# Queries stacked through DRAM instead of by transposes of split copies, with a new place for the first norm's statistics and the first score pair

## The reference

```
h = layernorm(x);  q = relu(h), k = v = relu(ctx)          # 16 heads of 32 features
att = softmax(q k^T / sqrt(32));  z = relu(att v @ ffn_w.T + ffn_b)
x1 = x + tanh(g_xattn) * z
n = layernorm(x1);  xr, xk = mixes of n and n shifted by one position (mu_r, mu_k)
y = sigmoid(xr @ W_r.T) * (relu(xk @ W_k.T)^2 @ W_v.T)
out = x1 + tanh(g_ffn) * y
```

## Time and profile before

| | us |
|---|---|
| median of 3 runs | 2914.57 (2912.64 to 2914.85) |
| the profiled execution's own time | 2913.12 |
| its span, first to last instruction | 2911.3 |
| steady time of one item | 44.20 |

### The profile page before, as it was taken

How to read it: one execution, slowest core, us unless ns; L and a number is a source line. 1 busy time by engine, 2 the same in 40 slices (tenths; PEclk the granted TensorE clock), 3 DMA queues, 4 the chain that set the end, 5 groups by cost and what they waited for, 6 DMA issues and landing times.

```text
span 2911.3 us, 71226 instructions
## 1 busy us (share of the span) xinstructions
PE 2792.9 (96%) x23042; PEld 2158.7 (74%) x23042; DVE 2367.5 (81%) x4173; ACT 1631.3 (56%) x2955; POOL 1055.1 (36%) x902
## 2 busy tenths in 40 slices
PE   4899999999999999999999999999999999999998
PEld 3677777777777777777777777777777777777776
DVE  5788888888888888888888888888888888888874
ACT  4555656556556555555556565565565555555552
POOL 0234334333333333343343343333333333333434
PEclk9999999999999999999999999999999999999999
DMA  5544544544544544545445445445445444454431
GB/s 183 151 142 133 158 140 132 159 140 135 152 145 131 157 132 142 149 131 152 142 130 159 139 133 159 139 135 152 143 132 157 132 144 146 132 154 141 130 112 43
DMA packets 405369, 408.83 MB, mean 140 GB/s; under 512 B 164560, under 2 KB 329424, under 8 KB 405328
## 3 DMA queue, kind: packets, MB, share of 16 engines
q1 hardware_dynamic: 353104, 341.17, 40.8%
q10 hardware_dynamic: 52224, 67.12, 6.6%
HBM read 272.90 MB, written 134.22 MB: 140 GB/s over the span
## 4 chain that ended last, share of the span: by engine, by line
PE 76%; DVE 16%; issue 5%; DMA 1%; SPq 1%; DVEq 1%; ACT 0%; POOL 0%; POOLq 0%; ACTq 0%
PE bank L955 41%; PE bank L922 8%; PE bank L936 7%; PE bank L948 7%; PE bank L910 6%; DVE m_nat L702 5%; DVE o_val L721 4%; PE bank L879 3%; DVE th L772 3%; PE bank L897 3%; DVE st L655 2%; PE bank L888 2%; DMA q_st<-m_t 0%; DVE mv L660 0%; DVE x L775 0%
## 5 line engine op out<-in xcount | busy, mean ns | idle before, releaser
L489 ACT ACTIVATE probs<-bank 128x512 f32<-128x512 f32 x1024 | 595.2, 592 | 439.1 <-PE bank L922 438.8
L702 DVE TENSOR_REDUCE m_nat<-bank 128x2 fp32r<-128x512 f32 x1024 | 700.2, 684 | 111.5 <-PE bank L910 110.8
L470 ACT ACTIVATE q_st<-bank 96x512 fp32r<-96x512 f32 x512 | 304.6, 595 | 583.2 <-PE bank L879 582.9
L721 DVE RECIPROCAL o_val<-bank 128x256 f32<-128x256 f32 x256 | 449.5, 1756 | 88.6 <-PE bank L948 82.3
L922 PE MATMUL bank<-q_st,k_st 97*128 97x256 f32 x2048 | 437.5, 295 | 14.0 <-DMA q_st<-m_t 13.9
L910 PE MATMUL bank<-k_st,q_st 96*128 96x256 f32 x2048 | 430.7, 292 | 5.5 <-DVE m_nat L702 4.6
L922 PEld LDWEIGHTS bank<-q_st,k_st 97*128 97x128 f32 x2048 | 345.8, 190 | 79.9 <-issue 26.9
L391 POOL TENSOR_TENSOR xm<-xm 128x512 f32<-128x512 f32 x128 | 144.9, 1132 | 711.0 <-ACT xm L533 711.0
L910 PEld LDWEIGHTS bank<-k_st,q_st 96*128 96x128 f32 x2048 | 357.5, 192 | 56.1 <-DVE m_nat L702 6.1
L711 DVE CAST m_t<-bank 4x256 fp32r<-4x256 f32 x256 | 105.3, 411 | 251.5 <-PE bank L888 251.5
L358 POOL TENSOR_TENSOR o_lo<-o_mv,o_hi 128x512 fp32r<-128x512 f32 x128 | 164.4, 1284 | 400.5 <-ACT o_hi L496 400.3
(11 more groups left out here) (88 smaller groups left out, 6042.3 us busy)
## 6 DMA issues: line engine op xcount, KB each, us to landing
k_st<-k_dram SPq DMA_DIRECT2D x256, 256.0 KB, 3.6
k_raw<-ctx_t_dram SPq DMA_DIRECT2D x256, 128.0 KB, 4.3
x_ln<-x_dram SPq DMA_DIRECT2D x256, 128.0 KB
k_dram<-k_high SPq DMA_DIRECT2D x64, 512.0 KB, 3.2
k_dram<-k_raw SPq DMA_DIRECT2D x64, 512.0 KB, 5.8
k_st<-k_dram SPq DMA_DIRECT2D x256, 128.0 KB, 3.5
o_dram<-o_val SPq DMA_DIRECT2D x256, 128.0 KB, 1.7
o_mv<-o_dram SPq DMA_DIRECT2D x512, 64.0 KB, 2.0
```

What stands on the lines that cost most here:

```text
L470: nc.scalar.activation(q_st[0:QK, c, :, P * u:P * u + P], tp_bank[0:QK, :].rearrange("p (g t) -> p g t", g=GR), ACT.Copy).then_inc(q_stack ...
L489: nc.scalar.activation(probs[:, n // GR % 2, n % GR, :, :].rearrange("p v t -> p (v t)"), st_bank[n % 2][:, :], ACT.Exp, scale=SCALE).then ...
L702: nc.vector.tensor_reduce(m_nat[:, c % 2, :, n % GR:n % GR + 1], s_bank[n % 2][:, :].rearrange("p (u y) -> p u y", u=NU), AX_X, ALU.max, n ...
L721: nc.vector.reciprocal(o_val[:, :], pv_bank[:, T:2 * T]).then_inc(rden_ready, 1)
```

## The change

Five things change.

1. **Queries.** `norm_1` writes `q_nat`, now plain float32 with 512 columns a half in an order that puts four heads' features side by side. `turn_q` transposes four blocks of 128x128 a turn, two turns an item (before: 8 turns of four blocks of 128x96), with no split ahead of it. `q_copy` on ScalarE copies a turn with the relu into `q_raw`, `q_halve` makes the high part for the whole item, `q_low` on VectorE the low part. `write_q` writes both to DRAM and `stack_q` reads each group back stacked, two DMAs a group, both issued on ScalarE's queue. `load_x` waits for `x_normed` instead of for the split.
2. **Statistics.** `stats_1(i+2)` moves from behind `head_max(i+1, 4)` to behind `head_max(i, 9)` (step 2), `norm_1` from item i+1 behind `head_max(i, 8)` to item i+2 behind `head_max(i, 11)`; `load_x` and `rstd_1` are an item further ahead, and the pipeline starts an iteration earlier. `k_low` moves from behind `head_max(i+1, 1)`, where `q_low` now is, to behind `copy_m(i+1, 0)`.
3. **Step 0.** Score pair 7 comes ahead of the first dense part on TensorE, `head_max(i, 7)` ahead of `finish` on VectorE.
4. **Maxima.** One transpose of 128x8 in place of two of 128x4; `m_t` has 8 rows of 128 in place of 4 of 256.
5. **The loop.** Seven iterations are written out ahead of the loop and seven behind it (before six and five).

```diff
@@ load_x
-                    after(sp, q_lo_ready, 2 * b)
-                    after(sp, q_hi_ready, 2 * b)
+                    after(sp, x_normed, NU * b)
@@ ScalarE, new functions (q_high and q_stack go)
+            def write_q(b, par):
+                    act.wait_ge(q_hi_ready, b + 1)
+                    act.wait_ge(q_lo_ready, b + 1)
+                    for half, tile in enumerate((q_high, q_raw)):
+                        act.dma_start(q_dram[par, :, half].rearrange("c f g t -> (f g) c t"),
+                                      tile[:, :, :]).then_inc(q_written, 16)
+            def stack_q(b, c, par):
+                    act.wait_ge(q_written, 32 * (b + 1))
+                    act.dma_start(q_st[0:HD, c, :, :].bitcast(F32), q_dram[par, c, 0]).then_inc(q_stacked[c], 16)
+                    act.dma_start(q_st[HD:QK, c, :, :].bitcast(F32),
+                                  q_dram[par, c].rearrange("h f g t -> (h f) g t")).then_inc(q_stacked[c], 16)
+            def q_copy(b, u):
+                    act.wait_ge(q_turned, NU * b + u + 1)
+                    after(act, q_written, 32 * b)
+                    nc.scalar.activation(q_raw[:, :, P * u:P * u + P], tp_bank..., ACT.Relu).then_inc(q_copied, 1)
+            def q_halve(b):
+                    act.wait_ge(q_copied, NU * (b + 1))
+                    nc.scalar.activation(q_high..., q_raw..., ACT.Copy).then_inc(q_hi_ready, 1)
@@ ScalarE, iteration: stack_q(i, 3) first, stack_q(i+1, 0..2) behind exponents 3, 7, 11,
   q_copy(i+2, 0..1) behind 6 and 8, q_halve behind 9, k_halve behind 10, write_q behind 13
@@ VectorE, norm_1
-                        nc.vector.tensor_scalar(x_ln[:, u, :], x_ln[:, u, :], mv..., rstd...,
+                        nc.vector.tensor_scalar(q_nat[:, u, :, :].rearrange("p c (f g) -> p c g f", g=GR),
+                                                x_ln[:, u, :].rearrange("p (c g f) -> p c g f", c=CH, g=GR), mv..., rstd...,
@@ VectorE, iteration
-                finish(i - 3, 1, 1 - par)
                 head_max(i, 7)
+                finish(i - 3, 1, 1 - par)
                 copy_m(i, 1)
@@ TensorE, turn_q and turn_m
-                    for g in range(GR):
-                        mm = nc.tensor.transpose(tp_bank[0:QK, P * g:P * g + P].bitcast(F32R),
-                                                 q_nat[:, u, GR * c + g, :, :], ident_r[:, :])
+                    for c in range(CH):
+                        mm = nc.tensor.transpose(tp_bank[:, P * c:P * c + P], q_nat[:, u, c, :],
+                                                 ident_r[:, :].bitcast(F32))
-                    for u in range(NU):
-                        mm = nc.tensor.transpose(tp_bank[0:GR, P * u:P * u + P].bitcast(F32R),
-                                                 m_nat[:, c % 2, u, :], ident_r[:, :])
+                    nc.tensor.transpose(tp_bank[0:GR * NU, 0:P].bitcast(F32R),
+                                        m_nat[:, c % 2, :, :].rearrange("p g u -> p (g u)"), ident_r[:, :])
@@ TensorE, iteration
-                turn(0)
                 shifted_scores(i, 0)
+                scores(i, 7)
                 dense(0, 0)
-                scores(i, 7)
                 values(i - 1, 3)
-                turn(1)
+                turn(0)
```

More of the change, by code:

```diff
@@ L138, in flamingo_block @@
         q_turned = sem("q_turned")
-        q_stacked = sem("q_stacked")
+        q_copied = sem("q_copied")
+        q_written = sem("q_written")
+        q_stacked = [sem(f"q_stacked{c}") for c in range(CH)]
         v_ready = sem("v_ready")
@@ L206, in pipeline @@
         def pipeline(eng, iteration):
-            for i in range(-2, 4):
+            for i in range(-3, 4):
                 iteration(i, i % 2)
-            with eng.Fori(6, NB // 2 + 3) as pair:
+            with eng.Fori(6, NB // 2 + 2) as pair:
                 iteration(pair * 2 - 8, 0)
                 iteration(pair * 2 - 7, 1)
-            for i in range(NB - 2, NB + 3):
+            for i in range(NB - 4, NB + 3):
                 iteration(i, i % 2)
@@ L561, in iteration @@
                 weights_split(i)
-                q_stack(i, 2, 1)
+                stack_q(i, 3, par)
                 exponent(i, 0)
@@ L595, in iteration @@
                 z_relu(i - 1, 0)
-                q_stack(i + 1, 0, 0)
+                q_copy(i + 2, 0)
                 exponent(i, 7)
+                stack_q(i + 1, 1, 1 - par)
                 split_high(i, 6)
-                q_stack(i + 1, 0, 1)
-                k_halve(i + 2)
                 exponent(i, 8)
@@ L611, in iteration @@
                 xt_copy(i - 1, 0)
+                q_halve(i + 2)
                 exponent(i, 10)
@@ L615, in iteration @@
                 xt_copy(i - 1, 1)
+                k_halve(i + 2)
                 exponent(i, 11)
-                q_stack(i + 1, 1, 1)
+                stack_q(i + 1, 2, 1 - par)
                 exponent(i, 12)
@@ L792, in iteration @@
                 relu_v(i, 0)
+                stats_1(i + 2)
                 head_max(i, 10)
                 split_low(i, 2)
-                q_low(i + 1, 0)
                 head_max(i, 11)
+                norm_1(i + 2)
                 split_low(i, 3)
@@ L825, in iteration @@
                 head_max(i + 1, 1)
-                k_low(i + 2)
+                q_low(i + 2)
                 head_max(i + 1, 2)
@@ L1103, in iteration @@
                 scores(i, 14)
-                turn(6)
                 dense(3, 3)
@@ L1109, in iteration @@
                 scores(i, 15)
-                turn(7)
+                turn(3)
                 dense(4, 1)
@@ L1123, in iteration @@
                 denominators(i, 1)
-                turn(10)
+                turn(6)
                 scores(i + 1, 1)
@@ L1141, in iteration @@
                 values(i, 2)
-                turn(12)
+                turn(7)
                 scores(i + 1, 4)
```

112 lines of the change are left out of this document (49 added, 63 removed).

## The result

The changed kernel takes 2840.24 us (median of 4 runs, 2835.96 to 2849.6), the kernel before, beside it, 2914.71 us (2912.64 to 2915.14). The ratio is 0.975, with a 95% interval of 0.9722 to 0.9778. The time fell by 74 us, where the prediction had 157 us and a range that ended at 2818. The profiled execution of after took 2835.96 us, with a span of 2834.2.

The account below looks back on a forecast made before the run. TensorE's matmul stream was taken as the bound: 60 steady items x (2.87 - 0.10) = 166 us, plus 6 at the ends, less 15 in the filling, gives -157 us, so 2757 us; range 2732 to 2818.

Parts of the forecast that it names:

- TensorE's sum: TensorE's matmul stream in a steady item: 2.56 - 0.90 + 0.24 + 1.00, taken as 2.87 us saved an item.
- the maxima: On TensorE, two transposes of 4 columns become one of 8, four times an item: 0.24 us saved.
- the query path: Query transposes on TensorE: 2.56 us go, 0.90 are added, 0.03 stay as slow start; 1.63 us saved an item.
- A query turn of four full transposes: On TensorE, one turn of four 128x128 fp32 transposes costs 0.45 us, two turns an item 0.90 us.
- The stall: TensorE's wait at step 0 for VectorE's maximum of head 7 should go entirely: 1.00 us an item.
- 0.45 us of margin: After the step 0 reordering, VectorE's maximum ends about 0.45 us before TensorE wants its transpose.
- VectorE and DMA at nothing: VectorE's changed work stays off the path but for 0.10 us; DMA share rises from 0.49 to 0.73, nothing added.
- VectorE rival: A thin VectorE margin breaks, leaving 0.5 to 1 us of wait an item: 45 us less gain, 2802 us; 24%.
- DMA rivals: The maxima's transfer q_st<-m_t lands late and TensorE waits: 2847 us (9%), or throughout at 7.07 us, 3020 us (5%).
- The filling: Before the steady items, queries go through DRAM and k_halve stands behind q_halve: 15 us lost, from 5 to 30.
- a wait of 0.10 us: At head maximum 3, VectorE's margin shrinks to 0.06 us, so 0.10 us of new wait is booked an item.

Follow-up runs that it names:

- two buffers: The changed kernel with a second buffer for o_val and two semaphores for its stores, the ones tile narrowed to make room: 2786.24 us, ratio 0.955.

## Why the prediction was wrong

*TensorE's sum: right, in part by luck.* 2.87 us an item was forecast. The floor fell by 2.82 us. Two of its terms were off and made up for each other: the maxima 0.24 for 0.35 us, the query path 1.63 for 1.50; where the missing 0.13 of the queries lies, no run shows. A query turn of four full transposes, forecast at 0.45 us, is 0.44 in after's chain, and the dense part behind it pays nothing (its usual 0.69):

```profile
1522.72 0.44 PE bank L890 x4
1523.16 0.69 PE bank L965 x3
```

*The stall: right where measured alone* (0.97 for 1.00), but it was costed as if nothing else depended on it. The prediction did ask what is late next on the way to the maximum, and found 0.45 us of margin; that margin held (no maxima's transpose on TensorE waits from 500 to 2500 us). It didn't ask the same of the instruction two places on, `norm_o`, whose hidden wait had the stall as its cover.

*VectorE and DMA at nothing: the step that failed.* The sentence is "The share of 0.73 shows that nothing is full on average, so I add nothing", and the place is the list of transfers on which anyone waits, which named the maxima's only. The share was forecast well (0.70 to 0.72). But the store that took 2.9 us at a share of 0.49 takes 4.4 us at 0.7 and up to 5.4, when 384 KB of queries are read at its side and the keys' writes stand closer. Three thinner things met: one buffer, a later landing, an earlier VectorE. This cost 54 us, 0.9 us an item; the filling's loss and what is left with two buffers, both below, make up the rest of the 83 us between 2757 and 2840. The VectorE rival had about the size of this one loss (45 us, 2802 us) and the wrong place: the maxima's transposes didn't wait. The maxima's transfer, the DMA rivals' bottleneck, held up no shifted pair from 500 to 2500 us in after.

*The filling: the term was too small.* +10.5 us was forecast to item 3 (15, less half of the saving in the first items) and 25.6 measured. The chain of after in the filling, the lines that answer to the earlier trace rows:

```profile
23.89 7.08 DMA k_dram<-k_raw
...
39.11 0.78 PE bank L920 x2
...
59.20 3.64 SPq L266
...
63.52 8.71 DMA q_st<-m_t
...
85.46 9.05 DMA q_st<-m_t
```

The first score pair comes 14.7 us later than the 24.44 of the earlier trace rows (10 to 13 were forecast). From there to the issue of the first maxima's move it is 24.4 us (18.6 before), much of it issues of 2 to 3.6 us each on SyncE that otherwise take 0.6; the two moves take 8.71 and 9.05 us (7.07 and 5.06). Together with 0.4 us of gain between them: 14.7 + 5.8 + 1.6 + 4.0 - 0.4 = 25.7. The prediction priced the new transfers by the old ones' durations, while the new ones lengthen the old too. TensorE's granted clock is lower as well behind this longer idling: 0.88 from 100 to 186 us, a mean between its two levels, against 0.96 in the same stretch before.

*What is left with two buffers*: the 60 items gain 150.0 us, not 166. The items from 3 to 5 take 43 to 45 us and not 41.43 (7.4 us in all), the last two 43.0 and 44.8 (4.9 us), and eight between them 41.5 to 43.0 (3.6 us). The floor of 41.43 us is no part of it: 44.20 - 2.77 is the same, though the forecast had a wait of 0.10 us in it that didn't come. Why the floor is 0.05 us over that of after is open. In the early items the projection waits for GpSimd's `o_low` (6.8 us in 140 to 450 us), behind the read of the stored quarters.

## What to carry to other kernels

- Before a stall is taken out, list every wait that stands behind it in program order on the same engine, also those that the profile shows at zero, with what each has in hand: for a single buffer that is stored, the time from the store's issue to the next write (4.2 us here) against the landing of that very store (2.9). A median over all stores of the tile, here 1.7, hides the one that counts. What a stall covered comes out when it goes.
- Added DMA traffic is not free while the mean share is below 1. Look at what is issued in the same microseconds as each short transfer that someone waits for: moving 384 KB of reads by some 5 us was worth 43.6 us here, and a second buffer of 1 KB a partition 54 us.
- Parts of a change that were measured alone don't add up in the whole: the reordered step was worth 58 us alone and 10 to 20 us beside the queries' traffic.

## What the runs showed of the hardware

A late VectorE made two of its own operations slower. `mix_r` (two SBUF operands) and `norm_1`, in after and, below, with two buffers (groups from 500 to 2500 us: count, busy us, mean ns):

```profile
L684 DVE TENSOR_SCALAR q_nat<-x_ln,mv,rstd 128x512 f32<-128x512 f32 x96 | 119.6, 1333 | 0.0
...
L777 DVE SCALAR_TENSOR_TENSOR xd<-xd,mu_sb,xt 128x256 f32<-128x256 f32 x188 | 100.8, 597 | 0.0
```

```profile
L685 DVE TENSOR_SCALAR q_nat<-x_ln,mv,rstd 128x512 f32<-128x512 f32 x96 | 87.1, 986 | 0.0
...
L778 DVE SCALAR_TENSOR_TENSOR xd<-xd,mu_sb,xt 128x256 f32<-128x256 f32 x192 | 79.8, 477 | 0.0
```

In the item at 1760 us GpSimd's square (line 393, 1767.69 to 1768.73) lies inside the `mix_r` that the wait had pushed there (1767.34 to 1769.81, 2.47 us for four in place of 1.9). So in this item the wait of VectorE cost some 0.5 us more than itself, right ahead of the maximum that TensorE wants. The Trainium skill ("GPSIMD Engine Reference", 1. Specifications) says that the two engines share SBUF interfaces and that VectorE instructions with two SBUF inputs contend there; `mix_r` agrees: in after the 74 of its 188 operations that overlap one of GpSimd take 783 ns in the mean, the others 476. `norm_1` has one tensor of input and grows beside GpSimd too: with two buffers the 18 of its 96 operations without a GpSimd operation beside them take 721 ns, the others 1047. What the two engines share in this case, the runs don't show.
